# Dense query projections, spread over 32-row head slots by transfers inside SBUF, in the attentions with 16-wide heads

## The reference

```python
# layer 0 (with a mask) and layer 2: cross-attention, x normalised first
q = split(xn @ Wq + bq); k = split(ctx @ Wk + bk); v = split(ctx @ Wv + bv)
attn = softmax(q @ k.T / sqrt(16) [+ mask * -1e9]); out = merge(attn @ v) @ Wo + bo
x = x + tanh(g) * out
# in the last feed-forward: self-attention over the 1024 tokens, no biases
q, k, v = split(layernorm(x) @ w_qkv); x = x + merge(softmax(q @ k.T / 4) @ v) @ w_proj
```

## Time and profile before

| | |
|---|---|
| median of 3 runs | 3254.08 us (3252.89 to 3259.18) |
| profiled execution | 3239.96 us |
| its span | 3238.0 us |
| DVE busy, ACT busy, POOL busy | 51%, 39%, 40% |
| `l0x` | about 4.9 to 151 us |
| `l0f` | from 152 us |
| `l2x` | from 1496 us; SP's first DMA there is issued at 1496.3 |
| `l3a` | 2476 to 3010 us |
| DVE in a unit of `l0x` | four reduces 1.85 us, shift 0.69, two 32x32 transposes 0.71 each, reciprocal 0.25, addition 0.48 |
| ACT, evacuation of 128x512 and exponential of 128x1024 | 0.69 us, 1.02 us |
| ACT begins to normalise in `l0x` | 12.76 us |
| slots cleared in `l0x` | 98 to about 135 us; 4992 + 2944 + 312 + 184 KB |

### The profile page before, as it was taken

The page is one execution under the profiler, slowest core; times in us unless marked ns, Lnnn a source line. Parts: engine busy times, 40 slices in busy tenths (PEclk is TensorE's granted clock), DMA queues, the critical chain, the costliest instruction groups (busy, mean ns, idle before and its releaser), DMA issues. The chain is left out here.

```text
span 3238.0 us, 41490 instructions
## 1 busy us (share of the span) xinstructions
PE 2950.1 (91%) x16033; PEld 1580.0 (49%) x16033; DVE 1641.4 (51%) x3315; ACT 1278.0 (39%) x1784; POOL 1286.4 (40%) x1025
## 2 busy tenths in 40 slices
PE   7998899999999999697988999978887899998898
PEld 3565344444434444244467889843333223322687
DVE  4625645654554465485651222156553877675400
ACT  4433344444344444355521111124333565555232
POOL 2332466665666566701244222215555310000433
PEclk9999999999999999898999999989998999999999
DMA  1500000000000000000026556420001000000386
GB/s 55 138 5 28 11 6 6 11 5 6 11 6 6 6 6 1 27 1 29 1 80 222 197 180 222 176 79 6 7 7 36 1 1 1 1 1 1 125 246 175
DMA packets 72758, 172.03 MB, mean 53 GB/s; under 512 B 17501, under 2 KB 52242, under 8 KB 59764
## 3 DMA queue, kind: packets, MB, share of 16 engines
q0 software_dynamic: 21744, 118.63, 10.7%
q1 hardware_dynamic: 50820, 50.75, 5.1%
HBM read 142.23 MB, written 27.64 MB: 52 GB/s over the span
## 5 line engine op out<-in xcount | busy, mean ns | idle before, releaser
L1520 POOL TENSOR_TENSOR l1x_added<-l1x_added,l1x_probs 128x1024 f32<-128x1024 f32 x224 | 527.2, 2354 | 264.5 <-ACT l1x_probs L1791 198.8
L1888 DVE TENSOR_REDUCE l1x_tops<-l1x_ring 128x1 f32<-128x512 f32 x512 | 326.6, 684 | 195.6 <-PE l1x_ring L1600 195.0
L1121 DVE TENSOR_REDUCE l3a_halves<-l3a_ring 128x1 f32<-128x512 f32 x512 | 324.7, 683 | 99.0 <-PE l3a_ring L966 94.9
L1791 ACT ACTIVATE l1x_probs<-l1x_slots 128x1024 f32<-128x1024 f32 x256 | 261.8, 1023 | 239.6 <-PE l1x_slots L1644 237.8
L1637 PE MATMUL l1x_slots<-l1x_Q,l1x_K 64*128 64x512 f32 x1152 | 310.9, 617 | 6.0 <-ACT l1x_probs L1789 4.8
L1082 ACT ACTIVATE l3a_probs<-l3a_slots 128x1024 f32<-128x1024 f32 x256 | 248.1, 1021 | 160.7 <-PE l3a_slots L986 160.7
L1659 PE MATMUL l1x_pv<-l1x_probs,l1x_V 128*64 128x512 f32 x1152 | 283.6, 608 | 0.0
L986 PE MATMUL l3a_slots<-l3a_Q,l3a_K 32*128 32x512 f32 x1024 | 150.0, 635 | 35.3 <-ACT l3a_probs L1082 34.5
L3527 DVE TENSOR_TENSOR l2f_hh<-l2f_sg,l2f_hid 128x256 f32<-128x256 f32 (+1 forms) x184 | 69.8, 380 | 217.2 <-ACT l2f_sg L3374 217.2
L3374 ACT ACTIVATE l2f_sg<-l2f_hid 128x256 f32<-128x256 f32 (+1 forms) x184 | 64.5, 351 | 280.6 <-PE l2f_hid L3290 278.3
L3290 PE MATMUL l2f_hid<-l2f_xgT,l2f_gate 128*128 128x256 f32 (+1 forms) x736 | 166.9, 349 | 2.3 <-ACT l2f_xgT L3361 1.5
(11 more groups left out here) (708 smaller groups left out, 5147.6 us busy)
## 6 DMA issues: line engine op xcount, KB each, us to landing
l1x_w<-in_l_qkv SPq DMA_DIRECT2D x16, 384.0 KB, 3.1
slots_in<-zeros SPq DMA_DIRECT2D x1, 4992.0 KB, 18.4
l2f_yg<-rows_out SPq DMA_DIRECT2D x8, 512.0 KB, 5.6
l2f_xg<-slots_in SPq DMA_DIRECT2D x15, 272.0 KB, 3.7
slots_in<-zeros SPq DMA_DIRECT2D x1, 2944.0 KB, 20.0
x<-in_x SPq DMA_DIRECT2D x4, 512.0 KB, 8.1
l1f_w<-in_l_w SPq DMA_DIRECT2D x2, 1024.0 KB, 7.1
x<-x SPq DMA_DIRECT2D x4, 512.0 KB, 2.9
```

Source lines behind the costliest of these rows:

```text
L1121: nc.vector.tensor_reduce(halves[:, k % 2, col:col + 1], bank_of(banks[e]), AX.X, ALU.max).then_inc(s["bank_done"], 1)
L1520: ins = nc.gpsimd.tensor_tensor(added[h][:], added[h][:], probs[:, n % PROBS, :, :], ALU.add)
L1791: ins = nc.scalar.activation(p, s2[m % 2], ACT.Exp)
L1888: ins = nc.vector.tensor_reduce(tops[:, e * NT + t, h:h + 1], bank, AX.X, ALU.max)
```

## The change

Queries are projected without padding: `pack16` gives dense weights, a projection (two matmuls 128x512) now gives eight heads, 16 rows each, and there are half as many. ACT evacuates into a dense tile. SP then copies, with four DMAs for each quad (16 rows x 512 tokens, 32 KB each), the rows of each head to rows 0 to 15 of its 32-row slot. The rows between (constants, ones) are no longer rewritten, so ACT fills the Q buffers (and K buffers in `self16`) once at the start of the stage. The shift writes a tile of its own, `lifted[u % 2]`, in place of Q. In `self16` keys are treated in the same way; in `cross16` they stay padded. New waits: the cast and the shift wait for the copies, ACT's next evacuation for the copies out of the dense tile, SP for the earlier readers of a Q (or K) buffer, the shift for the scores two units back. In `cross16` the bias load is moved ahead in SP's queue. The clearing of the slots is moved from the end of SP's program in `l0x` to that in `l0f`, after its weights have landed.

```diff
 def plan_cross:
     def query(u, pool=rings):
-        job("q", u, pool=pool)
-        events.append(("low", u))
+        if u % 2 == 0:
+            job("q", u, pool=pool)
...
             events += [("part", 0, u - 1), ("part", 1, u - 1)]
+        if u + 3 < units:
+            events.append(("low", u + 3))
 def cross16, SP:
+            sp.dma_start(bqk[:], w["bqk"]).then_inc(s["bias_loaded"], 16)
             sp.dma_start(cT[:], ...)
...
-            for rows, spare in to_clear:
-                sp.wait_ge(s["out_added"], CT)
...
+            for u in range(U):
+                sp.wait_ge(s["job_done"], done_by("q", u // 2 * 2))
+                if u >= QS:
+                    sp.wait_ge(s["shifted"], u - QS + 1)
+                    sp.wait_ge(s["low_ready"], u - QS + 1)
+                else:
+                    sp.wait_ge(s["pads_set"], QS)
+                for j in range(4):
+                    row = 64 * (u % 2) + 16 * j
+                    sp.dma_start(Q[u % QS][32 * j:32 * j + 16, :], dense[u // 2 % 2][row:row + 16, :]).then_inc(spread[u % QS], 16)
 cross16, POOL:
-                pool.wait_ge(s["job_done"], done_by("q", u))
+                spread_done(pool, u)
 cross16, ACT:
+            act.wait_ge(s["bias_loaded"], 16)
+            for i in range(QS):
+                nc.scalar.activation(Q[i][:].rearrange("p (a n) -> p a n", n=D), c.zeros[:].unsqueeze(1).broadcast_to([P, CH // D, D]), ACT.Identity,
+                                     bias=bqk[:, 10:11]).then_inc(s["pads_set"], 1)
...
+                    if u >= 4:
+                        spread_done(act, u - 4)
+                        spread_done(act, u - 3)
+                    ins = nc.scalar.activation(dense[u // 2 % 2][:], ps, ACT.Identity, bias=bqk[:, col:col + 1], scale=0.25)
 cross16, DVE:
-                dve.wait_ge(s["job_done"], done_by("q", u))
-                nc.vector.scalar_tensor_tensor(Q[u % QS][:], out, -1.0, Q[u % QS][:], ALU.mult, ALU.add)
+                spread_done(dve, u)
+                if u >= 2:
+                    dve.wait_ge(s["score_psum"], u - 1)
+                nc.vector.scalar_tensor_tensor(lifted[u % 2][:], out, -1.0, Q[u % QS][:], ALU.mult, ALU.add)
 def plan_self:
-    pieces = [v x 8] + [("q", 0, CH + i, 256) x 2] + [("k", 1, i * 256, 256) x 4] + [("q", 1, i, 256) x 2]
+    pieces = [v x 8] + [("q", 0, CH + i, 256) x 2]
...
-    for g in range(units // 2 - 1):
-        if g:
-            for i in range(2):
-                jobs[2 * g, 2 * i] = [("k", g + 1, i * CH, CH)]
-            jobs[2 * g, 4] = [("q", g + 1, 0, CH)]
-        jobs[2 * g + 1, 0] = [("q", g + 1, CH, CH)]
+    for g in range(1, units // 2):
+        at = (2 * g - 2, 1) if g == 1 else (2 * g - 2, 3)
+        lows[at] = [("k", g, 0), ("k", g, 1), ("q", g, 0), ("q", g, 1)]
+    for pair in range(1, units // 4):
+        u = 4 * pair - 4
+        jobs[u, 4], jobs[u, 5] = [("k", pair, 0, CH)], [("k", pair, CH, CH)]
+        jobs[u, 6], jobs[u + 1, 1] = [("q", pair, 0, CH)], [("q", pair, CH, CH)]
 def self16, SP:
+            def spread_heads(kind, g, h):
+                at = slice(h * CH, (h + 1) * CH)
+                sp.wait_ge(s["job_done"], part_done(kind, g // 2, h))
+                if g >= 2:
+                    sp.wait_ge(s["low_ready"], low_at[kind, g - 2, h])
+                    if kind == "k":
+                        sp.wait_ge(s["score_psum"], NT * (2 * g - 2))
+                    else:
+                        sp.wait_ge(s["shifted"], 2 * g - 3 + h)
+                else:
+                    sp.wait_ge(s["pads_set"], 4)
+                src, to = (dense_q, Q[g % 2]) if kind == "q" else (dense_k, K[g % 2])
+                for j in range(4):
+                    row = 64 * (g % 2) + 16 * j
+                    sp.dma_start(to[32 * j:32 * j + 16, at], src[row:row + 16, at]).then_inc(spread[kind, g % 2, h], 16)
+            for kind, g, h in (("q", 0, 0), ("k", 0, 0), ("k", 0, 1), ("k", 1, 0), ("k", 1, 1), ("q", 1, 0), ("q", 0, 1), ("q", 1, 1)):
+                spread_heads(kind, g, h)
+            for g in range(2, U // 2):
+                for kind in ("k", "q"):
+                    for h in range(2):
+                        spread_heads(kind, g, h)
 self16, ACT, ahead of everything else (zeros broadcast to 128x1024):
+            act.wait_ge(s["bias_loaded"], 16)
+            for i in range(2):
+                nc.scalar.activation(Q[i][:]..., zeros, ACT.Copy).then_inc(s["pads_set"], 1)
+                nc.scalar.activation(K[i][:]..., zeros, ACT.Identity, bias=bqk[:, 4:5]).then_inc(s["pads_set"], 1)
 def ffn0, SP, behind its weight loads:
+            for rows, spare in to_clear:
+                sp.wait_ge(s["w2_loaded"], 32)
+                sp.wait_ge(s["b2_loaded"], 32)
+                sp.dma_start(rows[:, 0:D]..., c.zeros...).then_inc(c.cleared, 16)
+                sp.dma_start(rows[:, D:], spare).then_inc(c.cleared, 16)
```

More of the change, by code:

```diff
@@ L330, in cross16, with spread_done @@
         x_loaded = [c.semaphore(f"{name}_x_loaded{n}") for n in range(NC)]
+        spread = [c.semaphore(f"{name}_spread{i}") for i in range(QS)]
         rows_total = 3 if mask is not None else 1
         block = ctx.enter_context(nc.Block())
+        def spread_done(eng, u):
+            eng.wait_ge(spread[u % QS], 64 * (u // QS + 1))
         def bank_free(eng, freed):
@@ L446, in project @@
                 for k in range(KD):
[L447 removed]
+                    last = nc.tensor.matmul(out, wq[:, k, q // 2 * P:(q // 2 + 1) * P], xT[:, k, n * CH:(n + 1) * CH], start=k == 0, stop=k == KD - 1)
                 last.then_inc(s["job_psum"], 1)
@@ L479, in scores @@
                     rows = slice(32 * j, 32 * j + 32)
-                    last = nc.tensor.matmul(slots[0:SC, j, :], K[rows, q, b * SC:b * SC + SC], Q[u % QS][rows, :], start=True, stop=True, tile_position=(32 * j, 0))
+                    last = nc.tensor.matmul(slots[0:SC, j, :], K[rows, q, b * SC:b * SC + SC], lifted[u % 2][rows, :], start=True, stop=True, tile_position=(32 * j, 0))
                 last.then_inc(s["score_psum"], 1)
@@ L764, in plan_self @@
                 job(*e)
-                if e[0] in ("q", "k") and (e[2] + e[3]) % CH == 0:
-                    low(e[0], e[1], e[2] // CH)
+            for e in lows.get((u, i), ()):
+                low(*e)
             for t in outs.get((u, i), ()):
@@ L833, in self16, with spread_done @@
         s = {n: c.semaphore(f"{name}_{n}") for n in names}
+        spread = {(kind, i, h): c.semaphore(f"{name}_{kind}_spread{i}{h}") for kind in "qk" for i in range(2) for h in range(2)}
         block = ctx.enter_context(nc.Block())
+        def spread_done(eng, kind, g, h):
+            eng.wait_ge(spread[kind, g % 2, h], 64 * (g // 2 + 1))
         def parts_of(u):
@@ L978, in scores @@
                     pe.wait_ge(s["shifted"], u + 1)
-                    pe.wait_ge(s["job_done"], max(part_done("k", g, 0), part_done("k", g, 1)))
+                    for half in range(2):
+                        spread_done(pe, "k", g, half)
                 if n:
@@ L1066, in evacuate @@
                 else:
-                    g, lo, wide = at
-                    q = g % QUADS
+                    pair, lo, wide = at
+                    if pair:
+                        for g in (2 * pair - 2, 2 * pair - 1):
+                            spread_done(act, kind, g, lo // CH)
                     if kind == "q":
-                        if g == 0:
-                            act.wait_ge(s["bias_ready"], 1)
-                        ins = nc.scalar.activation(Q[g % 2][:, lo:lo + wide], ps[:, 0:wide], ACT.Identity, bias=bqk[:, q:q + 1], scale=0.25)
+                        ins = nc.scalar.activation(dense_q[:, lo:lo + wide], ps[:, 0:wide], ACT.Copy, scale=0.25)
                     else:
-                        ins = nc.scalar.activation(K[g % 2][:, lo:lo + wide], ps[:, 0:wide], ACT.Identity, bias=bqk[:, 4 + q:5 + q])
+                        ins = nc.scalar.activation(dense_k[:, lo:lo + wide], ps[:, 0:wide], ACT.Copy)
                 ins.then_inc(s["job_done"], 1)
@@ L3591, in pack16 @@
         out[0, 16] = bo
-    packed = {"q": by_partition(padded(wq)), "k": by_partition(padded(wk)), "v": by_partition(wv), "o": by_partition(out.reshape(2 * D, D)),
-              "bqk": np.concatenate([b.reshape(4, P).T for b in bias], 1)}
+    packed = {"q": by_partition(wq), "k": by_partition(wk if dense else padded(wk)), "v": by_partition(wv), "o": by_partition(out.reshape(2 * D, D)),
+              "bqk": np.concatenate([b.reshape(4, P).T for b in bias] + [(zero if bq is None else bq).reshape(2, P).T, pads.reshape(4, P).T[:, 0:1]], 1)}
     if bv is not None:
@@ L3654, in program @@
         io["scratch"] = nc.dram_tensor("scratch", (TT, P), F32, kind="Internal").ap()
-        cross16(nc, c, "l0x", io["x"], weights(io, "l0x"), 0, io["ctx_t"], mask=io["mask0"], to_clear=[(io[f"slots_in{top}"], io[f"spare_rows{top}"]) for top in (2, 1)])
```

(3 more changed lines are left out.)

70 lines of the change are left out of this document (36 added, 34 removed).

## The result

| | median, us | lowest to highest |
|---|---|---|
| before (4 runs) | 3256.63 | 3252.89 to 3259.86 |
| changed (4 runs) | 3301.18 | 3291.51 to 3309.53 |

Ratio 1.0126, 95% interval 1.011 to 1.0142: by the ratio 41 us slower (the two medians are 44.6 apart). The forecast was 3241.5, its range ended at 3258. A second set of runs of the unaltered changed kernel on another occasion gave 3283.95 (3277.74 to 3293.81) against 3248.01: 1.0114 (1.0095 to 1.0133). The profiled execution of the first set took 3304.94, span 3303.2.

A forecast was written before the change was run, and what follows sets the result against it. TensorE, busy 91% of the span, was taken as the bound. l0x -2.9, l2x -2.1, l3a -15.9 + 3.2 and clock +5.1 gave -12.6 us, so 3241.5 us for the median of the runs; range 3225 to 3258.

The forecast's parts named there:

- Cross-attention, loop: l0x and l2x: eight queries fewer per stage, late maxima stall 1.3 us, pairs 13.72 for 14.24; -2.9 and -2.1 us.
- Self-attention, loop: l3a unit loop: projections fall from 25 to 12, three come into unit 0, no wait for copies; -15.9 us.
- Self-attention, prologue: l3a start: pad fills delay normalising 2.7 us, copies delay the maxima, VectorE then binds; +3.2 us, between +1.5 and +5.
- The copy: SP's four 32 KB copies: 3.1 us from evacuation to last landing (0.45 per issue, 1.7 landing), bounds 2.4 to 4.8.
- The clock: Cross stages' early units: new PE waits of 2 to 3 us bring three clock falls at 1.7 us each; +5.1 us.
- Rival B: Clock falls at every stall: twelve stalls, eight falls more than charged, +13.6 us, 3255, nothing gained; chance 0.14.
- rows 9: Trace of before: a 2.02 us PE wait in l2x, then clock 0.57 for 4 us; the same wait harmless in l0x.
- Cross-attention, prologue: Start of cross stages: first maxima 3 us late, one projection and a wait less; 0 us, between -1 and +1.
- Pad fills in `l2x`: Start of l2x: ACT fills four Q buffers before normalising, free at 1501.1 instead of 1500.3; +0.8 us.
- Clearing: Slot clearing, 8.4 MB moved from l0x to l0f behind its weights, with the queue otherwise unused; 0 us.
- Rival C: Slower by SP's copies between evacuation and cast in cross stages: 4.8 us per spread, +22, 3263.5; chance 0.11.
- Rival D: l3a gives half: the maxima's wait for VectorE replaces each removed projection, 8 us less gain, 3249.5; chance 0.1.

The follow-up runs named there:

- a4: a1 with the second pair's three projections (keys 0 and 1, first half of the queries) in self-attention's prologue instead of unit 0: 3233.24 us, 0.9954 of before.
- a2: Changed kernel with TensorE multiplying unused data in most waits for a spread query: 3268.25 us, ratio to before 1.0059.
- b1: Changed kernel with POOL's casts of odd units put back ahead of the scaling in the cross-attention loop: 3269.01 us, ratio to before 1.0062.
- a1: Changed kernel's self-attention alone, cross-attentions and clearing as in the kernel before: 3239.54 us, ratio to before 0.9968.
- c2: Kernel before with only the clearing of the slots moved from l0x to l0f: 3249.24 us, ratio to before 1.0007.
- a3: Changed kernel with the dense query projections of units 4 to 15 one unit earlier: 3269.66 us, ratio to before 1.0066.
- b2: a3 with POOL's casts at the head of each unit, ahead of the norm's columns and the scaling: 3244.65 us, ratio to before 0.9989.
- b3: b2 with a4's three projections in self-attention's prologue and each half of the pad fills behind a normalising: 3236.38 us, ratio to before 0.9963.
- c1: b3 with units 4 and 5's query behind unit 2's turn, and cross prologue queries ahead of the context's values: 3224.14 us, ratio to before 0.993.

## Why the prediction was wrong

The forecast was faster with 0.67; the kernel is slower, and by more than the range. What failed is the step *Cross-attention, loop*, forecast at -2.9 and -2.1 and measured at +22.1 and +18.5, with the clock term beside it: the casts' new place in POOL's order was put at nothing, and the falls of the clock at three. By the forecast's own steps:

- **Self-attention, loop, -15.9.** Right in kind, short by 3.7: 449.9 to 437.7 is -12.2. Units without projections take 26.43, as said; four of those that keep them took 0.4 to 0.5 us more each than before, and unit 0 took 6.6 more and not 3.76, as it started at half clock. In a4, with the three projections in the prologue, the loop is 431.1.
- **Self-attention, prologue, +3.2.** Measured +3.9. "The dropped pieces free only PE" was the flaw in the reasoning: freeing PE was not free, it took the clock (0.82, then 0.50). The price fell due in unit 0 and not here: a4's first shift comes at 46.2 too.
- **The copy, 3.1 us.** Measured 3.88 (3.84 in `l2x`): the four issues take 0.59 us each and not 0.45 (2.40 for four), the landing 1.9 and not 1.7. Inside the bounds given (2.4 to 4.8). With the terms of the forecast this is 13 x 0.8 = 10 us, most of the forecast gain. The section of the Trainium skill that was cited ("DMA: Bandwidth & Descriptors", Anatomy of one DMA) has about 2.0 us for the fixed cost, fitted on DMAs that GpSimd issues. These were issued by SP, a difference that the prediction left out; their landing, a median of 1.9 us here and of 2.0 in a2, is nearer to that figure than the 1.7 that I took from a load.
- **Cross-attention, loop, -2.9 and in `l2x` -2.1.** Measured +22.1 and +18.5. Four terms failed. (1) The copy, above. (2) A step of the diff was not costed: the casts' move behind the scaling on POOL. The prediction let the odd unit's query go by as free, because its copies land early; they do, but the cast waits for VectorE by way of the scaling. b1 puts 15 us on it in both stages together, with the clock falls at those waits in it. (3) The clock. (4) The odd query that was dropped had covered a wait for x: 2.84 us of idle in each stage where before has 0.66, 4.4 us for the two, and half clock behind it.
- **The clock, three falls x 1.7 = +5.1.** No term was further off in its count. It was taken as rare, since one of two waits of before had done it. In `l0x`'s loop of the changed kernel PE waited seven times for 2.0 us or more for the cast, and the granted clock of the next 4 us was 0.50 to 0.67 each time; after the waits of 1.12 and 1.31 it stayed 1.00. It is not a law: over both loops and both profiles of this kernel it fell behind 25 of 28 waits of 1.97 us or more, and stayed 1.00 behind one of 2.39. In the four profiles with the old cross-attention code (before, a1, a4, c2) it fell behind 3 of 8 waits of 2.0 to 2.1. At a mean clock of 0.83 and 0.85 the two loops lost at most 0.17 x 119.4 + 0.15 x 117.2 = 38 us of full speed, an estimate from above, since waits covered a part of it. Keeping PE busy in the waits gave back 16 us (a2), 11.5 of them in the loops, with part of the falls still there. Rival B had the mechanism ("the clock falls at every stall") at 0.14, but it counted twelve stalls, where the two stages have 23 waits for POOL's cast (21 of them behind the first shift; with those of the odd units, 22.7 and 24.6 us in all), and priced a fall at 1.7 us, where the late pair shows 2.3 net of what it covers. The rule of the Trainium skill that was cited ("TensorE: Matmul & The Clock Gate", Part 1) is that the throttled state is the default. It was the better guide here than the count from rows 9.
- **Cross-attention, prologue, 0.** Measured +6.0 in `l2x`, in both profiles: PE waits 2.6 us for the first cast, and at half clock the queries and values behind it take double. About 1 us of it is the wait and 5 the clock: in b1, a3, b2 and b3, with the same prologue, the clock stayed up and the stage's first shift came 0.9 to 1.4 later than before. With the order of c1 the wait itself is gone.
- **Pad fills in `l2x`, +0.8.** Not seen: normalising starts 4.1 us after the stage's start, 4.0 before. In `l3a` normalising begins 6.1 after the stage's start where it began 3.9 after, 2.2 late, forecast 2.7.
- **Clearing, 0.** Right (c2).

By these sizes: 6 paths a stage x 0.8 and one in `l3a`, +10; the casts' place on POOL about +15; the clock at least +16 by a2, in part in a prologue where it may be chance. On the forecast of -12.6 that is +28, of the 36 and 45 us measured in the two sets of runs. It is no clean sum, as b1's 15 hold clock falls too and a slow clock hides the odd unit's wait. One late pair of units takes the terms apart: forecast 13.72; 14.20 in b1, with the longer copy and the clock up; 15.12 in a2, with the odd unit's wait besides; in the changed kernel, with the falls, 16.6 in the mean of four and 17.45 in the one shown. Which of the two, the order or the clock, cost more over the whole stages stays open.

Rival C named the copies' latency and decided from 4.1 us; it stayed at 3.9. It had the place right, the copies between evacuation and cast, and not the price: a spread of 3.9 alone would have left the change some 2.5 us ahead (12.6 - 10.1). Rival D did not come: the loop of `l3a` gave 12.2 of 15.9, and the missing part lies in unit 0 and in units that keep projections.

## What to carry to other kernels

When work is taken off the bound engine and replaced by a path through a DMA, lay the whole new path on a timeline, with the order of the instructions on every engine it passes: here an instruction moved by a few lines in POOL's order cost 15 us, with the slow work that its waits brought. Start the path early enough that nothing waits for it (the late units of b2), and see what the removed work had covered: a wait for x, and TensorE's clock. An idle of 2 us on TensorE is to be priced as the idle plus a good chance of slow work behind it, and work that stands beside another engine's bound is not to be cleared away.
